# Attention on one core: row maxima eleven key steps ahead instead of twelve, and a new order of three queues around the maximum rows

## The reference, cut to what matters

```python
x = x + attention(layernorm(x))          # 16 heads of 16, rotary, softmax, projection; x is (4, 1024, 256)
x = x + cross_attention(ctx, ctx, layernorm(x))   # 77 keys
x = x + experts(x)                       # 8 experts, 512 tokens each, top-k by gate, scatter back

# inside attention, the stage that the change is in
attn = jnp.einsum('bhqd,bhkd->bhqk', q, k) * scale
attn = jax.nn.softmax(attn, axis=-1)
out = jnp.einsum('bhqk,bhkd->bhqd', attn, v)
```

## Time and profile before

| | |
|---|---|
| median of 3 runs | 1172.51 us (1167.86 to 1174.52) |
| the profiled execution | 1171.57 us |
| its span, first to last instruction | 1169.8 us |
| TensorE busy | 1067.4 us, 91% |
| VectorE busy | 1004.3 us, 86% |
| ScalarE busy | 768.2 us, 66% |
| GpSimd busy | 533.2 us, 46% |
| mean granted TensorE clock | 0.947 |

### The profile page before, as it was taken

How to read it: one execution, slowest core, us unless ns; L and a number is a source line. 1 busy time by engine, 2 the same in 40 slices (tenths; PEclk the granted TensorE clock), 3 DMA queues, 4 the chain that set the end, 5 groups by cost and what they waited for, 6 DMA issues and landing times. The chain is left out here.

```text
span 1169.8 us, 23180 instructions
## 1 busy us (share of the span) xinstructions
PE 1067.4 (91%) x8508; PEld 593.6 (51%) x8508; DVE 1004.3 (86%) x2108; ACT 768.2 (66%) x932; POOL 533.2 (46%) x866
## 2 busy tenths in 40 slices
PE   7888899999999999999999999988983069999998
PEld 6775333333333333333333333357773048888897
DVE  8999799999999999999999999436998975666653
ACT  4552288888888888888888888944555024555653
POOL 2747944554545454544445523232200023766665
PEclk9997599999999999999999999989996559999999
DMA  6787823232322333232313220045522022554443
GB/s 242 254 259 228 188 42 80 54 75 45 83 49 63 60 69 64 58 65 55 79 44 80 53 53 18 16 139 181 193 90 95 0 86 70 141 148 116 112 113 36
DMA packets 90141, 114.03 MB, mean 97 GB/s; under 512 B 31105, under 2 KB 62833, under 8 KB 90033
## 3 DMA queue, kind: packets, MB, share of 16 engines
q1 hardware_dynamic: 66872, 69.57, 20.0%
q0 software_dynamic: 19824, 36.48, 15.5%
q10 hardware_dynamic: 3336, 6.56, 1.6%
HBM read 73.31 MB, written 38.27 MB: 95 GB/s over the span
## 5 line engine op out<-in xcount | busy, mean ns | idle before, releaser
L834 DVE TENSOR_REDUCE b_max_halves<-banks 128x1 f32<-128x512 f32 x1024 | 624.4, 681 | 12.9 <-PE banks L881 12.8
L759 ACT ACTIVATE b_probs<-banks 128x1024 f32<-128x1024 f32 x512 | 520.7, 1027 | 130.9 <-PE banks L912 130.9
L881 PE MATMUL banks<-b_k,b_q 62*128 62x512 f32 x1024 | 393.5, 467 | 9.1 <-DVE b_max_halves L834 2.9
L912 PE MATMUL banks<-b_q,b_k 64*128 64x512 f32 x1024 | 380.0, 454 | 4.9 <-issue 4.4
L897 PE MATMUL banks<-b_probs,b_v 128*17 128x256 f32 (+1 forms) x3840 | 314.7, 400 | 0.2 <-ACT b_probs L759 0.2
L912 PEld LDWEIGHTS banks<-b_q,b_k 64*128 64x128 f32 x1024 | 159.9, 185 | 234.4 <-issue 185.9
L881 PEld LDWEIGHTS banks<-b_k,b_q 62*128 62x128 f32 x1024 | 165.6, 190 | 36.8 <-DVE b_max_halves L834 33.6
L897 PEld LDWEIGHTS banks<-b_probs,b_v 128*17 128x17 f32 x3840 | 63.9, 95 | 162.4 <-issue 95.7
L483 POOL DMA_DIRECT2D b_q<-q_stacks x120 | 62.6, 529 | 75.3 <-DMA b_q<-b_max_rows 61.9
L1612 POOL DMA_INDIRECT e_x<-rows,d_idx x32 | 45.3, 1416 | 110.6 <-DVE d_wx L1787 57.1
L1832 DVE TENSOR_TENSOR e_hTl<-e_hT,e_hTh 128x512 fp32r<-128x512 f32 x64 | 47.7, 745 | 48.6 <-ACT e_hT L1586 48.6
(11 more groups left out here) (264 smaller groups left out, 1623.0 us busy)
## 6 DMA issues: line engine op xcount, KB each, us to landing
e_w<-in_w SPq DMA_DIRECT2D x16, 1024.0 KB, 7.6
q_stacks<-a_parts SPq DMA_DIRECT2D x32, 256.0 KB, 3.9
k_stacks<-a_parts SPq DMA_DIRECT2D x32, 256.0 KB, 4.1
b_q<-q_stacks POOLq DMA_DIRECT2D x60, 128.0 KB, 3.2
b_k<-k_stacks POOLq DMA_DIRECT2D x30, 256.0 KB, 4.3
v_tiles<-a_v ACTq DMA_DIRECT2D x8, 544.0 KB, 3.6
b_rec_spread<-reciprocals SPq DMA_DIRECT2D x128, 32.0 KB, 1.9
attended<-b_att SPq DMA_DIRECT2D x128, 32.0 KB, 1.7
```

The source lines that it names most:

```text
L759: nc.scalar.activation(pr[:, S % NP, u], ps[:, 2 * u:2 * u + 2, :], ACT.Exp, scale=D ** -0.5).then_inc(s_ex[u], 1)
L834: v.tensor_reduce(mxp[:, (k // NB) % 2, s, p, t, kh:kh + 1], ps[:, bank(k), :], AX.X, ALU.max)\
L881: nc.tensor.matmul(ps[:, bank(k), :], qs[g][stack, h, p, P * t:P * t + P], ks[g][stack, p, CH * kh:CH * kh + CH], start=True, stop=True).t ...
L912: return nc.tensor.matmul(ps[:, 2 * u + s, :], ks[g][stack, u, P * kt:P * kt + P], qs[g][stack, h, u, :], start=True, stop=True)
```

## The change

```diff
@@ attend
-        AHEAD = 12 * PER
+        AHEAD = 11 * PER
-        LATE = AHEAD // PER - KT
+        LATE = 2 * KT - AHEAD // PER
@@ SyncE, start of the stage
             ones(0)
-            end_stores(sp)
             sp.wait_ge(s_ra, 1)
             rows(sp, 0, 0, (0,))
             ones(1)
+            end_stores(sp)
@@ SyncE, each half
                     if back:
                         tail.sums(sp, m, x)
-                        tail.inverted(sp, m, x)
-                    if hg > 1:
-                        tail.store(sp, m - 1, i, (hg - 2) // 2, 1 - x)
-                    elif not first:
-                        tail.store(sp, m - 1, i - 1, NG - 1, 1 - x)
                     if not (last and hg == NH - 1):
                         sp.wait_ge(s_ra, NH * i + hg + 2)
...
+                    if back:
+                        tail.inverted(sp, m, x)
+                    if hg > 1:
+                        tail.store(sp, m - 1, i, (hg - 2) // 2, 1 - x)
+                    elif not first:
+                        tail.store(sp, m - 1, i - 1, NG - 1, 1 - x)
                     if back:
                         tail.spread(sp, m, x)
@@ GpSimd, start of the stage
             pool.wait_ge(s_minus, 1)
-            end_sums(g_, pool)
...
                 if g == 1:
                     load(0, 1)
+                    end_sums(g_, pool)
@@ GpSimd, each half
-                    if back:
-                        tail.refine(pool, g_, step, 8 * i + hg - 1, (hg - 1) % 2)
                     if back and more:
...
                         rows(pool, (hg + 1) // 2 % NG, (hg + 1) % 2, (1,), s_row2)
+                    if back:
+                        tail.refine(pool, g_, step, 8 * i + hg - 1, (hg - 1) % 2)
```

## The result

Before has a median of 1172.49 us (1167.86 to 1176.61), after 1179.78 us (1175.47 to 1186.22), 15 runs each. The ratio is 1.0063, 95% interval 1.0047 to 1.0078: the change costs about 7.3 us, a loss that is small and clear of the noise. The forecast was 1171.0, a gain of 1.5.

A forecast was written before the change was run, and what follows sets the result against it. VectorE and TensorE were taken as both almost full in mid-stage, maxima setting the pace. Terms -6.8 + 0.5 + 3.0 + 2.2 - 1.5 - 0.4 + 1.5 = -1.5 us gave 1171.0 against the median 1172.51; 8-in-10 range 1164 to 1181.

The forecast's parts named there:

- The turn one step later: In 31 halves: 4.29 us left for the rows, ordinary turns free, odd landings and GpSimd's pauses late: +3.0 us.
- rival A: At `rows_in` on TensorE: rows late at every half, 30 times, making the kernel slower; 1183 at 0.4 us each; chance 0.16.
- The second half's rows: Eight row DMAs on one queue at the second half: TensorE waits 2.4 us less 0.2 of slack, +2.2 us.
- My clock term: Clock rise behind the first scores: nearly moves along with the earlier scores, +0.5 us.
- The start: Start of the attention stage: four maxima fewer and rows no longer late, first scores at 128.9 for 135.7: -6.8 us.
- the prediction's own sign: At the start of the stage: the prediction is wrong if first scores stay behind 133 us.
- Rows ahead of inversion and store: Within each half: the transposition no longer waits for GpSimd's `parts` behind a late `refine`, -1.5 us.
- The last maxima: Last halves: two more iterations at 1.22 us cost 0.5, waits of about 0.9 go: -0.4 us.
- End of the stage: SyncE's sums, inversion and whole list in the last half come 1.5 us later, delaying the next stage: +1.5 us.

The follow-up runs named there:

- e12: The changed kernel (after) with `AHEAD` at 12 steps in place of 11 and nothing else; 1168.65 against 1171.36 us, ratio 0.9974.
- e6: The changed kernel with `AHEAD` at ten steps in place of eleven; 1283.70 against 1172.31 us, ratio 1.0951.
- e4: The changed kernel, with GpSimd waiting behind its first sum until VectorE's first transposition; 1178.05 against 1172.56 us, ratio 1.0051.
- e3: The kernel before with only the order within a half changed, rows ahead of inversion and store; 1169.94 against 1172.56 us, ratio 0.9985.
- e7: The changed kernel with twelve steps, both new orders kept, and GpSimd's sums held until the first turn; 1164.74 against 1172.31 us, ratio 0.9934.
- e2: The kernel before with eleven steps ahead alone, all queues in the old order; 1180.64 against 1172.56 us, ratio 1.0073.
- e5: The changed kernel with four of the second half's eight row DMAs moved from SyncE's queue to GpSimd's; 1173.49 against 1172.31 us, ratio 1.0009.
- e11: The changed kernel with inversion and store ahead of the rows again in the last half but one alone; 1177.91 against 1171.36 us, ratio 1.0038.
- e1: The kernel before with only the start's order changed: group loads first, last sums and stores behind; 1168.41 against 1172.56 us, ratio 0.9972.
- e9: The kernel before with only SyncE's twelve last projection stores moved behind the first rows; 1169.93 against 1171.50 us, ratio 0.9983.
- e10: The changed kernel with sums held until the first turn and the second half's rows shared with GpSimd; 1177.37 against 1171.50 us, ratio 1.0054.

## Why the prediction was wrong

**Where the sum broke.** After and e12 differ in `AHEAD` alone, so the pieces of their two profiles show what the step costs, in us: the first exponential -2.9 (29.60 against 32.47), the first half +2.3 (23.82, 21.54), the second +2.3 (22.16, 19.85), the next 28 +6.5 (561.01, 554.47), the last but one +0.8 (18.45, 17.64), the end of the block +1.7 (5.91, 4.19). That is +10.8, with the stage's own start (105.63, 103.20) and the later stages (1.5 shorter in after) left out. The prediction had for these -2.4, and +2.2, 3.0 and some 1.5 of costs, +4.3 in all.

In the pieces of before and after, the forecast's -1.5 became +8.6 of span: the stage began 3.0 later, the start won 2.1 less, the first two halves cost 0.9 more (the late turn behind the second), the 28 halves 3.2 more, the last half but one 0.7, the end 1.4, and the later stages took 1.1 off. (Rounding leaves 0.1.)

**The turn one step later (+3.0 forecast; 7.4 by the turns' lateness).** This is the step that failed most. The length that is free was right: 4.29 us forecast, 4.29 to 4.32 seen. The landing was right: 4.0 forecast, 3.95 to 4.01 seen, and e6 shows it by itself. Two things were wrong. I let the rows come 4.4 us behind the turn, by a slack of VectorE's behind TensorE's own ("so the rows may come at 4.4"), and there is none: a landing at 4.60 made TensorE begin at 4.66 and the half 20.17 us long, all 0.36 beyond 4.30. And I took five odd landings and two pauses from the trace of before as what the new program would have; after has twelve. The landings aren't random: after, e4 and e6 have the same order of instructions, and in all three GpSimd's rows land beyond 4.1 us behind the turns 5, 7, 10, 15, 20, 21, 25, 29 and 31 (counted from 0), though e6 comes to them up to 100 us later. In before they were seven (10, 11, 13, 15, 22, 29, 30), with e3's order alone twelve, and twelve again in e7 and e12. So the new order moved them to other turns and made more of them; with twelve steps ahead the 2.4 us of cover hide them (e3's halves take 19.81), with eleven each shows. The two errors can be told apart: before's own seven, counted without the slack, make 4.4 us in place of my 3.3, and the rest up to 7.4 are late turns that before hadn't. For a loss as such the second error isn't needed: e2 keeps the old order and has seven late turns, 5.3 us of them by the same count.

What makes a landing late was not tested, but a count over the 30 turns behind the second half's in all fourteen profiles narrows it. GpSimd pauses between its row DMAs at 27 of these 420 turns. At the others its rows landed in time 282 times and beyond 4.1 us 111 times. All 111 have a transfer of 8 or 16 KB of an instruction queue (q8 or q14) that begins 1.5 to 3.9 us behind the turn, while the rows are under way; of the 282 only 5 have one. That is a coincidence in the traces, if a close one; no kernel removed those transfers, so it is not shown as the cause.

This is rival A's place and sign, but not its mechanism: A had the rows late at every half, and here 18 of 30 turns are in time. Nor is its arithmetic met. In my sum 7.4 in place of 3.0 makes the total +2.9, and the rest up to +7.3 came from the other terms.

**The second half's rows (+2.2).** Right: a wait of 2.25 us. What I missed is what follows: behind it the mean granted clock was 0.66 over 5 us, the second half grew by 2.3 us (0.9 of it the late turn behind it), and e5, which halves the wait, has no such fall. My clock term, +0.5, was put at the first scores, where it was 0: 132 to 136 at 0.50 and 136 to 144 at 0.60, the rise some 9 us behind the first scores in both kernels. That the two terms together, 2.7, are just what the first two halves lost without the late turn (1.3 + 2.3 - 0.9) is luck. The 0 is luck too: over the fourteen kernels the rise came 6.4 to 9.6 us behind the first scores. An iteration at the lower level took 2.14 us (TensorE's weight loads at 159.47 and 161.61 in after), a little less than the twice 1.22 of the forecast. e6 has the fall behind most of its turns. A wait doesn't always bring it: at turn 10 TensorE begins late alike in after and in e11 (landings at 6.27 and 6.13 us), and the clock falls behind it in e11 alone, where the next half takes 21.30. The Trainium skill (TensorE: Matmul & The Clock Gate, Part 1) ties the clock to how busy the array has been; the trace agrees in that within the stage the clock fell only behind a wait.

**The start (-6.8).** The rows are no longer late, and e4 has the whole 6.8 (2.4 of four maxima and the 4.4 of waiting). After has 4.7: I had moved GpSimd's sums to the time of VectorE's `parts` and not asked what two engines do beside each other. L667 took 2.19 to 2.20 us in all six kernels with the new start and no hold (after, e1, e5, e6, e11, e12), and 0.17 to 0.18 in the other eight, where no sum of GpSimd's ran beside it. It ended each time within 0.05 us of the end of GpSimd's sum. VectorE's maximum of two inputs just ahead of it did the same when it met the sum before: 0.71 us in e12, 2.01 in e11. The reading of the maxima, with its one input in the banks, took 0.64 beside the sums (e1) as without them (e7). The cast between, one input in place of two, took 0.17, but it began within 0.03 us of a sum's start, so it says little. The Trainium skill (GPSIMD Engine Reference, 1. Specifications) says that GpSimd shares its way to SBUF with VectorE and that they contend where VectorE has two SBUF inputs; the trace agrees, and has the size, 2.0 us, which is what was left of GpSimd's sum. Of what had held the rows before, e9 takes the stores out: 1.2 us; by e9's landings the loads hold them for the rest. Moreover the whole stage began 3.0 us later in this profile. In all profiles with SyncE's stores moved the first maximum is read at 103.2 to 106.1, in before, e2 and e3 at 102.1 to 102.6; four issues of the projection's stores ahead of it take 6.14 us in after and 4.51 before:

```profile
93.57 6.14 SPq L165 DMA_DIRECT2D k_stacks<-a_parts  x4
```

These stand ahead of everything that was moved. The cause is open. By the prediction's own sign, first scores behind 133 us, it was wrong here too: they started at 133.3, 3.0 of it with the stage's late start.

**Rows ahead of inversion and store (-1.5).** Right in size, by e3. But e2, with the old order, has no late `refine` in mid-stage either (its transposition waits for `parts` once, 0.7 us): with eleven steps `parts` come later, and the order has nothing left to win there. The term belongs to twelve steps and was counted in a sum for eleven.

**The last maxima (-0.4).** +0.3 in the last half but one: the last turn is one of the twelve late ones.

**End of the stage (+1.5).** 2.9. The spread ended 11.4 us behind the turn, since the store's four DMAs ahead of it took 3.31 us where I had the ordinary 1.81, and the sums stood 6.0 us into the last half (760.67 to 766.69) in place of 3.5. e11 puts inversion and store ahead of the rows again and has 2.08. How much of it reaches the end is less plain, the later stages were 1.1 shorter.

**The sum of the parts.** By the ratios the start alone is worth -3.3 us (e1), the order alone -1.8 (e3), eleven steps alone +8.6 (e2): +3.5. Each is known to 1.6 to 2.2 us either way. Both orders with twelve steps are -3.0 (e12), with the hold -7.7 (e7), and eleven steps on top of the orders make +7.4. So eleven steps cost 8.6 in the old order and 10.4 in the new, a difference within the noise. The profiles put it at the end of the block (5.91 against e2's 2.15) and in the late turns.

## What to carry to other kernels

The lead that hides a transfer must be as long as its landing. Count the free length against the worst landings and not the ordinary one, and take slack on an engine that is 99% busy as zero. Late landings recur at the same turns of one program and move when the order of its instructions changes, so the trace of before gives their size and not their number. And when work is moved on one engine, look at what the others do at its new time: here a sum on GpSimd made a 0.18 us instruction on VectorE take 2.2, and each mend shifted the next wait (e10, e11).

## What the hardware showed that was not expected

- A VectorE subtraction of 128 by 16 with two inputs stood for 2.19 to 2.20 us beside GpSimd's sums of 128 by 1024, until the sum's end, where it takes 0.18 alone; reductions with one input from the banks took their usual 0.64.
- A wait of TensorE of 2.25 us was followed by a mean granted clock of 0.66 over 5 us; one of 2.6 us by 0.81 and 0.76 over the two stretches of 4 us at and behind it (e6).
- Small DMAs of GpSimd's, otherwise 1.7 to 1.8 us to their landing, took up to 2.6 (2.8 in before) at turns that are largely the same in kernels with the same order of instructions. At all 111 such turns in fourteen profiles a transfer of an instruction queue begins 1.5 to 3.9 us behind the turn, and at 5 of 282 ordinary ones.
- GpSimd paused for 1.48 us between two of four DMA issues at the same turn (10) in every kernel but those that issue four of the second half's rows from GpSimd (e5, e10), and for 1.0 us at turn 29 in all fourteen.
